# A Mamba, mixture-of-experts and linear-attention kernel: the first unit's preparation done inside the routing program, scores turned round, scatters spread over two units

## What is computed

```python
xn = _layernorm(x)
s = _L0_attn_ref(xn, ...)          # two-directional Mamba, 512 inner channels, 16 states
g = _silu(_L0_ffn_ref(xn, ...))    # 8 experts, the best 2 of each row
x = x + s * g
xn = _layernorm(x)
s = _L1_attn_ref(xn, ...)          # linear attention, then three MLP levels
g = _silu(_L1_ffn_ref(xn, ...))
return x + s * g
...
# one direction of the Mamba; the other runs on the reversed sequence
x = x * conv_w + conv_b (depthwise, 4 taps); x = _silu(x)
x_dbl = x @ Wx.T
dt = softplus(x_dbl[..., :64] @ Wdt.T + bdt);  B, C = the last 2 x 16 columns
carry = exp(dt * A[n]) * carry + dt * B[n] * x          # for each n of 16 states, over 512 steps
y = sum over n of carry * C[n], plus x * D, times _silu(z)
```

## Time and profile before

| what | us |
|---|---|
| median of 3 runs | 3166.66 |
| lowest and highest run | 3166.04, 3168.67 |
| the profiled execution, whole | 3172.15 |
| its span | 3170.4 |
| routing block, up to the last DVE instruction | 83.7 |
| first state of unit 0 on POOL | 147.5 |
| last scan of unit 15 ends | 2109.5 |
| attention block starts | 2140.7 |

### The profile page before, as it was taken

One profiled execution on the slowest core, in us unless ns is written; L12 is line 12 of the kernel. 1 busy time (PEld: TensorE's weight loads), 2 busy tenths in 40 slices (PEclk: granted clock), 3 DMA queues, 4 the chain that ended last, 5 costly groups with the idle time before them and its releaser, 6 DMA issues. The chain is left out here.

```text
span 3170.4 us, 40091 instructions
## 1 busy us (share of the span) xinstructions
PE 2612.1 (82%) x13342; PEld 1723.8 (54%) x13342; DVE 2253.1 (71%) x2790; ACT 1776.4 (56%) x2731; POOL 1738.3 (55%) x550
## 2 busy tenths in 40 slices
PE   5357788787787887878878878657999999999999
PEld 5134565565565565565555555545556455555554
DVE  5399999989989989989989989984343442442430
ACT  1367777767867958858858858522332332332322
POOL 0598879869878878878778788851000000000000
PEclk9777899899999989989989989767999999999999
DMA  6223333333334333324333333213000000000000
GB/s 254 84 77 120 111 110 116 133 117 118 111 115 141 115 107 122 131 88 145 112 103 126 136 107 118 70 53 116 26 33 0 33 33 0 33 33 0 7 7 7
DMA packets 144229, 274.85 MB, mean 87 GB/s; under 512 B 23095, under 2 KB 94238, under 8 KB 143006
## 3 DMA queue, kind: packets, MB, share of 16 engines
q1 hardware_dynamic: 137886, 255.70, 23.7%
q0 software_dynamic: 6144, 16.79, 1.6%
HBM read 231.80 MB, written 40.63 MB: 86 GB/s over the span
## 5 line engine op out<-in xcount | busy, mean ns | idle before, releaser
L745 POOL TENSOR_TENSOR hs<-u,bb 128x2048 f32<-128x2048 f32 x256 | 1159.0, 4536 | 288.4 <-PE hT L1087 249.0
L947 DVE TENSOR_TENSOR_SCAN hs<-dA,hs 128x1024 f32<-128x1024 f32 x512 | 1163.1, 2278 | 96.5 <-POOL hs L745 72.6
L1087 PE MATMUL hT<-ident,hs 128*128 128x128 f32 x3616 | 586.3, 304 | 362.2 <-DVE held L957 312.1
L842 ACT ACTIVATE dA<-dt,cols 128x511 f32<-128x511 f32 x1024 | 661.4, 680 | 318.0 <-DVE hs L947 313.0
L1087 PEld LDWEIGHTS hT<-ident,hs 128*128 128x128 f32 x3616 | 443.5, 154 | 521.8 <-DVE held L957 370.5
L957 DVE SCALAR_TENSOR_TENSOR held<-hT,ct,held 128x512 f32<-128x512 f32 x872 | 604.5, 733 | 22.7 <-PE hT L1087 22.1
L1361 ACT ACTIVATE gl<-bank,cols_sb 128x512 f32<-128x512 f32 x192 | 130.7, 687 | 527.1 <-PE bank L1600 526.8
L1600 PE MATMUL bank<-mT,cms_sb 128*128 128x512 f32 x768 | 362.6, 597 | 10.1 <-ACT mT L1355 8.6
L138 POOL COPY cur<-slot 128x8 uint32 (+1 forms) x8 | 1.5, 190 | 626.7 <-DVE held L150 626.2
L1106 PEld LDWEIGHTS moe<-xgT,held 128*128 128x128 f32 x2272 | 289.0, 205 | 54.3 <-issue 26.4
L1106 PE MATMUL moe<-xgT,held 128*128 128x128 f32 x2272 | 302.9, 290 | 13.0 <-ACT xgT L857 13.0
(11 more groups left out here) (232 smaller groups left out, 3295.6 us busy)
## 6 DMA issues: line engine op xcount, KB each, us to landing
held<-wl SPq DMA_DIRECT2D x71, 1024.0 KB
bb<-b_scratch SPq DMA_DIRECT2D x128, 512.0 KB
held<-wl SPq DMA_DIRECT2D x71, 512.0 KB
xg<-xg_scratch SPq DMA_DIRECT2D x71, 128.0 KB
yg_scratch<-yg SPq DMA_DIRECT2D x71, 128.0 KB, 1.7
held<-x SPq DMA_DIRECT2D x16, 512.0 KB, 8.6
xg_scratch<-zero SPq DMA_DIRECT2D x8, 1024.0 KB, 4.7
cb<-b_scratch SPq DMA_DIRECT2D x30, 256.0 KB, 4.4
```

Of the source, the lines that this page charges most:

```text
L745: nc.gpsimd.tensor_tensor(hs[n % HS][:, :, :], u[d][:, :, :], row, ALU.mult).then_inc(dBu_ready, 1)
L842: last = nc.scalar.activation(dst, src, ACT.Exp, scale=cols[:, at:at + 1])
L947: nc.vector.tensor_tensor_scan(h, decay, h, 0.0, ALU.mult, ALU.add).then_inc(scan_done, 1)
L1087: last = nc.tensor.transpose(hT[c % 2][:, k * P:(k + 1) * P], hs[n % HS][:, k, c * P:(c + 1) * P], ident[:, :])
```

## The change

The weights of the Mamba layer are loaded between the batches of x. Unit 0's preparation moves from the start of the second block into the routing block, piece by piece between the batches. Its convolution taps are made by POOL (8 products) where DVE made them, and ACT makes the copies that DVE made half of. The scores are computed with `w_r`, padded to 32 columns, as the stationary operand and 512 turned rows streaming; four batches share one bank, ACT copies it and PE turns it back, in two halves. Choosing and weights are done by half, and the log-and-sum step of unit 0 (`soft`) comes at the end of DVE's routing list.

The 36 early indirect DMAs become 16: three chunks each after the states 0 and 1 of unit 0, two after state 2. One chunk follows each later state of unit 0 and each of the states 0 to 10 of unit 1. DVE's wait for the early ones moves ahead of its first `weigh`. SP loads the first two tiles at state 11 of unit 1. Unit 1 no longer gives states 2 and 9 to POOL. The tiles move four places later: unit 1 has one tile, in slots 25 to 30, and each later unit has five, unit 15 as well.

```diff
--- before.py
+++ after.py
-T0 = 5
+TPU = TPB // 2
+FIRST_TILE = (1 - TPB, 1 - TPU)
-        EARLY = 18
+        EARLY = 8
+        OPEN = 3
+        GROUPED = 11
...
+        def turned(unit, n):
+
+            if in_first_batch(unit):
+                return NS * unit + n
...
+        def by_pool(unit):
+
+            return () if in_first_batch(unit) else POOLN
...
+                load_x(0)
+                sp.dma_start(w_r[:, :, 0:NE], w_rT.rearrange("(k p) m -> p k m", p=P)).then_inc(wr_in, 16)
+                sp.dma_start(rows[:, :, :], rows0.partition_broadcast(P)).then_inc(wr_in, 16)
+                load_x(1)
+                sp.dma_start(w_in[:, :, :], w_inT.rearrange("(k p) m -> p k m", p=P)).then_inc(w_in_in, 16)
+                load_x(2)
+                for g in range(2):
+                    for half in range(2):
+                        sp.dma_start(w_tap[HP * half:HP * (half + 1), g, :], cols0[HP * g:HP * (g + 1), CW:CB]).then_inc(taps_in, 16)
+                load_x(3)
+                sp.dma_start(cols[:, :], cols0).then_inc(first_in, 16)
+                for d in range(2):
+                    sp.dma_start(w_x[:, d, :, 0:RX], w_xT[d].rearrange("(k p) m -> p k m", p=P)).then_inc(first_in, 16)
+                sp.dma_start(w_dt[0:R, :, :], w_dtT.rearrange("d r m -> r d m")).then_inc(first_in, 16)
+                for b in range(4, NB):
+                    load_x(b)
                 sp.wait_ge(gz, 1)
                 flat = xg_dram.rearrange("(p r) d -> p (r d)", p=P)
                 for i in range(N_ZERO):
...
+                root(2)
+                turned_rows(1)
+                act.wait_ge(edges, 4)
+                piece("proj", 0)
+                root(3)
+                turned_rows(2)
+                piece("proj", 1)
+                root(4)
...
+                turned_rows(6)
+                piece("conv", 3)
+                turned_rows(7)
+                piece("silu", 0)
+                scores_out(1)
+                a_cols = cols[:, AL:AL + 2 * DB * NS]
+                nc.scalar.activation(a_cols, a_cols, ACT.Exp).then_inc(setup_a, 1)
+                shares(0)
+                piece("xd", 0)
+                piece("dt", 0)
+                piece("dt", 1)
+                shares(1)
+                piece("c", 0)
+                piece("dt", 2)
+                piece("dt", 3)
+                prepare_copies(act, "soft", 0, 0, 0, 0, None, True)
...
+                choose(0)
+                choose(1)
+                weights(0)
...
+                weights(1)
+                dve.wait_ge(setup_a, 1)
+                a_cols = cols[:, AL:AL + 2 * DB * NS]
+                nc.vector.tensor_scalar(a_cols, a_cols, -1.0, None, ALU.mult)
+                for quarter in range(4):
+                    soft(dve, 0, 0, quarter)
...
-                def scores(b):
-                    for c in range(NC):
-                        for k in range(KD):
-                            last = nc.tensor.matmul(bankR[7][:, (NC * b + c) * NE:(NC * b + c + 1) * NE],
-                                                    xaT[b % 2][:, k, c * P:(c + 1) * P], w_r[:, k, :],
-                                                    start=(k == 0), stop=(k == KD - 1))
...
+                    g, h = b % QB, b // QB
+                    for k in range(KD):
+                        last = nc.tensor.matmul(bankR[4 + h][RG * g:RG * (g + 1), :], w_r[:, k, :], xT(b)[:, k, :],
+                                                start=(k == 0), stop=(k == KD - 1))
+                    if g == QB - 1:
+                        last.then_inc(sc_ps, 1)
...
+                pe.wait_ge(g0, 3)
+                turn_rows(0)
+                turn_rows(1)
+                pe.wait_ge(wr_in, 32)
+                scores(0)
+                pe.wait_ge(w_in_in, 16)
+                piece("proj", 0)
+                turn_rows(2)
+                scores(1)
+                piece("proj", 1)
+                turn_rows(3)
+                scores(2)
+                pe.wait_ge(taps_ready, 8)
+                piece("conv", 0)
+                piece("proj", 2)
+                turn_rows(4)
+                scores(3)
+                piece("conv", 1)
+                piece("proj", 3)
...
+                turn_rows(7)
+                scores(6)
+                scores(7)
+                turn_scores(1)
+                pe.wait_ge(g0, 10)
+                pe.wait_ge(first_in, 16 * 4)
+                piece("xd", 0)
+                piece("dt", 0)
+                piece("dt", 1)
+                pe.wait_ge(chosen, 2)
                 flat = ms[:, :, :].rearrange("p c e -> p (c e)")
-                nc.tensor.matmul(bankR[5][:, 0:TC * NE], before[:, :], flat, start=True, stop=True)
-                nc.tensor.matmul(bankR[6][:, 0:TC * NE], ones[:, :], flat, start=True, stop=True).then_inc(cnt_ps, 1)
+                nc.tensor.matmul(bankR[4][:, 0:TC * NE], before[:, :], flat, start=True, stop=True)
+                nc.tensor.matmul(bankR[5][:, 0:TC * NE], ones[:, :], flat, start=True, stop=True).then_inc(cnt_ps, 1)
+                piece("c", 0)
+                piece("dt", 2)
+                piece("dt", 3)
...
-            def tile_pieces(d, last):
+            def tile_pieces(d, first):
                 out = {s: [] for s in range(2 * NS)}
-                for i in range(-T0, 0) if d == 0 else range(NT - TPB * (NB - 1) if last else TPB - T0):
+                for i in range(1) if first else range(FIRST_TILE[d], FIRST_TILE[d] + TPU):
                     for at, piece in enumerate(("x", "a", "", "b", "gate", "down")):
-                        out[starts[i + T0 if d == 0 else i] + at].append((piece, i))
+                        out[starts[i - FIRST_TILE[d]] + at].append((piece, i))
...
-                            if n == NS - 2 and unit_is_first(unit):
+                            if n == GROUPED and unit_is_first(unit - 1):
 
                                 sp.wait_ge(grouped[0], 16 * 2 * EARLY)
                                 sp.wait_ge(grouped[1], 16 * 2 * (TC - EARLY))
...
-                pool.wait_ge(placed, 1)
-                pool.wait_ge(zeroed, 16 * N_ZERO)
-                for c in range(TC - EARLY, TC):
-                    group(c, grouped[0])
+
+                def groups(unit, n):
+
+                    if unit_is_first(unit):
+                        return range(TC - EARLY, TC)[3 * n:3 * n + 3] if n < OPEN else (n - OPEN,)
+                    return (NS - OPEN + n,) if unit_is_first(unit - 1) and NS - OPEN + n < TC - EARLY else ()
...
-                            if not later(unit) and n < TC - EARLY:
-                                group(n, grouped[1])
+                            if in_first_batch(unit) and d == 1 and n == POOLN[-1] + ADD[d][-1]:
+                                add_skip(unit)
+                            for c in groups(unit, n):
+                                group(c, grouped[int(c < TC - EARLY)])
...
-                for s in range(2 * NS):
-                    for what, k in PREP[0][s]:
-                        prepare(what, k, 0, 0, 0, True)
-                act.wait_ge(setup_v, 1)
...
                     if n == 0 and c == 0:
                         dve.wait_ge(p_used, use_of("c", 0, d, unit) + 1)
+                        if unit_is_first(unit):
+                            dve.wait_ge(grouped[0], 16 * 2 * EARLY)
```

610 lines of the change are left out of this document (317 added, 293 removed).

## The result

The changed kernel takes 3147.38 us, the median of five runs (3142.91 to 3152.73), where the kernel before, run beside it, takes 3167.60 (3166.04 to 3170.44). The ratio is 0.9937 with a 95% interval of 0.9926 to 0.9948: 20.2 us less, and by the interval 16 to 23 less. The forecast was 27.5 us less (3139), the range 3123 to 3162: the time lies in the range, 8.4 us above the forecast, and the gain is 7 us smaller than forecast. The profiled execution took 3148.03, its span is 3146.3; before, 3172.15 and 3170.4.

What follows compares the result with a forecast made beforehand. DVE was taken to bound the kernel to about 2140 us, PE after. Terms -58 + 14 + 5 - 6.5 + 0.5 + 0.5 + 17 = -27.5, from the median 3166.66 to 3139; range 3123 to 3162.

Steps and rivals of the forecast that it cites:

- The bound: Whole kernel: DVE is full from the routing to about 2140 us, PE after; only the path ahead of 2140 counts.
- Term 1: Routing block and unit 0's preparation: the first state starts at 89.5 us instead of 147.5, -58.
- the margin of 3: Routing block: 3 us added to the first state's time for unexplained ACT waits of 2 to 4 us seen before.
- rival (b): Routing block does not close up, through ACT's waits or PE's lower clock between pieces: 15 us more, 3154; chance 0.19.
- Rival (c): PE stays at the lower clock level through the whole routing block: first state near 124, time 3173; chance 0.07.
- Term 2: Opening of unit 0: with scatters between states, scan 3 starts about 40 us after the first state, before 26.4; +14.
- Term 3: Seam between units 0 and 1: scatter pairs behind states 14 and 15 of unit 0 delay POOL, 2 x 2.56; +5.
- Term 4: Unit 1: fewer tile gates and no wait for POOL's additions, against two more states on DVE; net -6.5.
- rival (d): Scatters beside scans take as long as the scan, 2.28 us: 22 x 1.3 more in unit 1, 3168; chance 0.02.
- Term 5: Unit 15 with five tiles: three more gates fit in DVE's wait for POOL's additions; +0.5.
- Term 6: End of unit 15: the gather waits for the last tile's store, so `moe_chunk` starts 17 to 19 us later; +17.
- rival (a): End of unit 15: the gather's wait does not decide, only +7 of PE's pieces is left: 3129; chance 0.14.

Runs made afterwards that it cites:

- e3: Changed kernel with POOL's tap products made later, four after the third batch is normalized and four after the last: 3143.63 us, ratio 0.9917.
- e4: Changed kernel with only the turned-round scores undone: narrow products straight into the bank, no copy and turning back: 3142.83 us, ratio 0.9917.
- e6: The changed kernel as it stands, timed and profiled a second time: 3149.85 us, ratio 0.9936 to the kernel before.
- e7: Changed kernel with all 16 early scatters in one row ahead of unit 0's first state, not behind states 0, 1 and 2: one run, 3146.30 us.
- e8: Changed kernel without the 26 scatters behind states 14 and 15 of unit 0 and 0 to 10 of unit 1: one run, 3141.12 us.
- e2: Changed kernel with unit 15's five tiles starting every fifth slot (0, 5, 10, 15, 20): 3144.91 us, ratio 0.9915.

## Why the prediction was right, point by point

**The bound.** That the path ahead of 2140 us decides and that the loop keeps its pace is what the table shows: units 2 to 14 moved by -0.9 and +2.3, inside what variants of one kernel differ by. (That DVE was busy nine tenths or more in nearly every slice up to 2140 us is said too strongly: of the 25 slices from the third on, seven show an 8.)

**Term 1**, -58 forecast, -57.1 and -55.5 measured, is right in size by two errors against each other. The rebuilt list gave the end of DVE's list as 85.7 without the margin of 3. The last score came at 60.8 instead of 57.5, the rows were placed at 79.8 instead of 75.3, and the log-and-sum step ended at 89.9 instead of 85.7, so the whole error is in PE's rounds and in the turning back; choosing, weights, counts and placing took what they were given. Two steps failed there. "The eight tap products move to POOL ... so about 11 us for what DVE did in 5.5" counted only POOL's time (8.87 measured) and not what they do to DVE: 3.2 us, shown by e3. And turning back was given 1.5 us at the end and nothing in the middle, where it took 2.5 at the end and 3.3 in the middle with 1.2 of lower clock behind it: e4 prices the form of the scores at 3.6 net against the old one. The margin I had put there for ScalarE's waits paid for these; ScalarE held PE up once in the rounds, for the copy of the scores (2.25 us), and not 2 to 4 us a few times as rival (b) supposed. Rival (c) did not come: from 25.57 on turns took 1.04 to 1.09 and pairs 1.90 to 1.98, but for the one behind the gap (3.11). So the size came out right by luck, two costs left out against a margin set for another cause, and the same block in e6 gives -55.5.

**Term 2**, +14, measured 38.8 - 26.4 = +12.4. The first weighing, which waits for the early rows, started at 125.76, 35.3 us after the first state instead of 37, and ran beside the fourth state. e7 shows that it is POOL's work and not its order. **Term 3**, +5, is confirmed to a tenth by e8 (5.0). Terms 2 and 3 together are +17.9 for +19 by the table.

**Term 4**, -6.5, measured -4.3 and -5.2. DVE's busy time fell from 110.55 to 109.59, where the sum had +0.4. The waits that were to go came to 7, and they went nearly as forecast: 5.21 for POOL's additions is gone, and what DVE waited for turns fell from 2.84 to 1.84. But its idle time fell only from 10.9 to 7.6, because the wait for the unit's first state, behind the pairs of term 3, rose from 1.89 to 4.62. Leaving that wait at its old size is the step that failed. e8, without the pairs, has it at 1.92 and still takes 116.3 us for the unit: DVE then brings more work over from unit 0 (busy 111.97 in this window instead of 109.59), so the pairs' price is all in the stretch before. What the prediction named as "what is late next", POOL's list with the scatters, held DVE up nowhere behind the seam, and PE had no wait for the tile loaded late in the unit.

**The scatters beside the scans.** They took 0.96 in units 0 and 1, with 1.19 the longest in this kernel, so rival (d) fell. The Trainium skill's figure of 3100 ns that the prediction weighed (SBUF — State Buffer, "SBUF: two separate sides") stands there for a DMA beside a VectorE copy from SBUF to SBUF. It did not come up in these units, where DVE ran nothing beside the 64 scatters but scans and weighings, each with one operand in PSUM; whether it would beside such a copy no run here shows.

**Term 5**, +0.5, measured +1.3 and +2.3, is small and was put too low: nine profiles with these tile places have 122.3 to 123.3 us for the unit, before it took 121.0. What makes the 1 to 2 us is not shown. **Term 6**, +17, measured +14.1 and +14.3, is the term over-sized: the pieces of the last tile cost the weighs 3.9 us (S + 12.9 for S + 9.0) and not 7. PE's second products took 1.89 + 0.69, where 3.22 + 0.7 up to 5.0 had been taken from rows at the lower level, and the last turns and weighs were quicker too; everything behind them shifted by that. The mechanism is as forecast: a chain of store (S + 11.3), gathers (from S + 14.2, 9.9 us) and landing, with DVE idle 10.09; e2 shows that it is the gather's wait that ends last; rival (a) had only PE's work left there.

**The sum.** Up to `moe_chunk` the forecast was -27.5 and the two profiles have -29.0 and -23.8, and whole they have -24.1 and -18.9; the difference is the first batch of the attention block, +5.2 and +4.3. The prediction took this block as unchanged; its instructions are, and its time follows the granted clock, in variants from -1.4 to +5.4 around that of before. The medians have -20.2, and the time lies 8.4 us above the forecast. Of these, 3.4 are what the first profile misses (24.1 for 27.5). The other 5 were in no term: the prediction took 5.5 off because the profiled execution of before lay that far above its median, and the changed kernel's lies 0.7 above its own. With five runs before instead of three that distance is 4.6. Such an offset belongs to one execution and does not carry over. Whether the changed kernel falls on the low side of the clock more often than others is not settled.

## What to carry to other kernels

When work moves to an idle engine, price what it does to the engines beside it, not only its own time: the tap products saved DVE 5.5 us of its own and blocked it for 3.8. A transformation that makes one engine's instructions look cheaper has to be priced at the clock level at which they will run; 3.58 and 1.85 us are the same 16 products. A short wait can cost more than itself, as the 2.25 us at 46.45 did. And a transfer that gathers what the last stored piece holds wants that piece early: two or three slots moved in one unit were worth 8.4 us at the end.
